# One cross attention of a twelve-layer decoder, rewritten as a single block with a turn per batch

## The reference, cut to what matters

```python
x = x + _L0_xattn_ref(_layernorm(x, axis=-1), ctx_768, L0_xattn_Wq, L0_xattn_Wk, L0_xattn_Wv, L0_xattn_Wout, L0_xattn_bout)

def _L0_xattn_ref(x, context, Wq, Wk, Wv, Wout, bout):
    HEADS = 8
    DIM_HEAD = 64
    SCALE = DIM_HEAD ** (-0.5)
    b, n, _ = x.shape
    m = context.shape[1]
    q = (x @ Wq).reshape(b, n, HEADS, DIM_HEAD)
    k = (context @ Wk).reshape(b, m, HEADS, DIM_HEAD)
    v = (context @ Wv).reshape(b, m, HEADS, DIM_HEAD)
    sim = jnp.einsum('bihd,bjhd->bhij', q, k) * SCALE
    attn = jax.nn.softmax(sim, axis=-1)
    out = jnp.einsum('bhij,bjhd->bihd', attn, v).reshape(b, n, HEADS * DIM_HEAD)
    return out @ Wout + bout
```

## Time and profile before

| what | us |
|---|---|
| median of 3 runs | 1572.71 (1567.17 to 1577.11) |
| profiled execution, whole time | 1575.55 |
| its span, first to last instruction | 1573.8 |
| PE busy in the span | 1303.9 (83%) |
| DVE, ACT, POOL busy | 730.2, 517.6, 405.9 |
| mean granted TensorE clock | 0.868 of full speed |
| stretch of the changed layer | 99.5 to 197.9 |

### The profile page before, as it was taken

The page is one execution under the profiler, slowest core; times in us unless marked ns, Lnnn a source line. Parts: engine busy times, 40 slices in busy tenths (PEclk is TensorE's granted clock), DMA queues, the critical chain, the costliest instruction groups (busy, mean ns, idle before and its releaser), DMA issues. The chain is left out here.

```text
span 1573.8 us, 26994 instructions
## 1 busy us (share of the span) xinstructions
PE 1303.9 (83%) x10492; PEld 950.1 (60%) x10492; DVE 730.2 (46%) x2172; ACT 517.6 (33%) x1216; POOL 405.9 (26%) x435
## 2 busy tenths in 40 slices
PE   4978839799968756887787799998959999983998
PEld 4866628588833433664465597785637774562676
DVE  4543374343479354663475414526841126655111
ACT  4523313344355312332342211312423324331332
POOL 5922288000053224740672120003010001030000
PEclk9998859899976676998898857998969989885999
DMA  3000040421091000000000000000021100000010
GB/s 126 1 4 0 0 174 1 132 70 55 2 279 36 1 29 0 1 1 1 0 1 1 8 2 1 1 3 2 1 73 40 40 12 1 3 1 27 28 40 27
DMA packets 46542, 48.28 MB, mean 31 GB/s; under 512 B 18944, under 2 KB 37888, under 8 KB 45536
## 3 DMA queue, kind: packets, MB, share of 16 engines
q1 hardware_dynamic: 46432, 46.76, 9.5%
HBM read 41.91 MB, written 4.85 MB: 30 GB/s over the span
## 5 line engine op out<-in xcount | busy, mean ns | idle before, releaser
L1156 PE MATMUL bank<-xnT,scratch 128*128 128x512 f32 x256 | 117.0, 606 | 15.6 <-DMA scratch<-e_l_ffn_w 15.6
L1217 DVE SCALAR_TENSOR_TENSOR x_res<-bank,scratch,x_res 128x128 f32<-128x128 f32 x128 | 36.0, 344 | 195.0 <-PE bank L1167 195.0
L1167 PEld LDWEIGHTS bank<-scratch 128*128 128x128 f32 x1024 | 118.1, 192 | 11.5 <-issue 11.5
L1196 ACT ACTIVATE scratch<-bank 128x512 f32<-128x512 f32 x128 | 76.5, 597 | 143.1 <-PE bank L1156 143.1
L1167 PE MATMUL bank<-scratch 128*128 128x128 f32 x1024 | 118.2, 275 | 0.0
L1156 PEld LDWEIGHTS bank<-xnT,scratch 128*128 128x128 f32 x256 | 48.0, 195 | 67.4 <-issue 66.4
L862 ACT ACTIVATE scratch<-bank 128x512 f32<-128x512 f32 x96 | 52.6, 594 | 93.7 <-PE bank L763 93.6
L821 DVE TENSOR_REDUCE scratch<-bank 128x4 f32<-128x512 f32 x96 | 63.1, 685 | 40.7 <-PE bank L2416 22.9
L2648 PE MATMUL bank<-weights,xnT 128*128 128x512 f32 x64 | 43.9, 787 | 23.7 <-DVE scratch L2757 21.4
L2641 POOL TENSOR_TENSOR scratch<-scratch 128x16 f32<-128x16 f32 x16 | 51.6, 3227 | 39.5 <-DVE scratch L2790 39.5
L827 DVE TENSOR_TENSOR scratch<-bank,scratch 128x512 f32<-128x512 f32 x96 | 61.3, 679 | 0.0
(11 more groups left out here) (527 smaller groups left out, 2896.3 us busy)
## 6 DMA issues: line engine op xcount, KB each, us to landing
scratch<-conv_kernels SPq DMA_DIRECT2D x8, 1024.0 KB, 11.0
scratch<-e_l_ffn_w SPq DMA_DIRECT2D x32, 256.0 KB, 2.8
scratch<-e_l_ffn_w SPq DMA_DIRECT2D x4, 1024.0 KB, 13.9
values<-scratch SPq DMA_DIRECT2D x8, 512.0 KB, 2.6
scratch<-values SPq DMA_DIRECT2D x8, 512.0 KB, 4.3
weights<-w_l_ffn SPq DMA_DIRECT2D x1, 3698.0 KB, 11.5
weights<-w_l_attn SPq DMA_DIRECT2D x1, 2560.5 KB, 9.0
weights<-w_l_attn SPq DMA_DIRECT2D x1, 2048.0 KB, 10.9
```

The costliest lines, as they stand in the source:

```text
L1156: nc.tensor.matmul(ps[m % 4][:, :], wa[s][:, i * P:(i + 1) * P], core.xnT[:, half * BANK:(half + 1) * BANK], start=True, stop=True) \
L1167: mm = nc.tensor.matmul(ps[4 + half][:, t * P:(t + 1) * P], hT[half][:, i, t * P:(t + 1) * P], wb[s][:, i, :], start=(i == 0), stop=(i == ...
L1196: nc.scalar.activation(hT[half][:, i, :], ps[m % 4][:, :], act_func, bias=bias2[:, s, i:i + 1] if b1 is not None else 0.0) \
```

## The change

The layer becomes one block with its own order, `NormInBlock` for the norm, and a turn per batch. Keys of the first four batches are projected first, from the context, while the norm runs; keys of the other four are projected one chunk a turn, queries of a pair in two fills, values of a batch in one fill with a column of ones beside each head. All fills, the output projection and the transposed output go through the two banks 4 and 5 in a fixed sequence, and ACT empties them in the same sequence. The output bias is laid out over 128 partitions on the host and added to x by POOL, which also adds each batch's projected output to x. The classes and functions that only the old form used are gone. Batch 0's values are in the opening list and, by `ahead(-1)`, once more in turn -1. Nothing else in the program changes.

```diff
-    layernorm_all(core, tag)
-    attention_by_pairs(core, tag, c, names_of(4, False, 4), heads, make, wq, wk, wv, wo, core.ctxT, CTX,
-                       K ** -0.5, bo=bo)
+    S_BANKS, T_BANKS, F_BANKS, O_BANKS = (0, 1), (2, 3), (4, 5), (6, 7)
...
+    TURNS = range(-1, B + 2)
+    first = [("k", 0, i) for i in range(CH)] + [("v", 0), ("q", 0, 0), ("q", 0, 1)]
+
+    def ahead(n):
+
+        fills = [("q", (n + 3) // 2, (n + 3) % 2)] if n + 3 < B else []
+        fills += [("k", 1, n + 1)] if n + 1 < CH else []
+        return fills + ([("v", n + 1)] if n + 1 < B else [])
...
+        @block.gpsimd
+        def _(pool):
+            nc.gpsimd.memset(vaug[:, :, :, K:K + 1], 1.0).then_inc(ones_set.sem, ones_set.up())
+            for h in range(2):
+                norm.pool(pool, h)
+            pool.wait_ge(*core.w_loaded[tag])
+            for h in range(2):
+                pool.wait_ge(norm.xn.sem, norm.batch(norm.xn, B // 2 * (h + 1) - 1))
+                xs = core.x[:, B // 2 * h:B // 2 * (h + 1), :]
+                nc.gpsimd.tensor_tensor(xs, xs, bo.unsqueeze(1).broadcast_to([P, B // 2, D]), ALU.add) \
+                    .then_inc(biased.sem, biased.up())
+            for b in range(B):
+                pool.wait_ge(biased.sem, biased.at(b // (B // 2)))
+                pool.wait_ge(emptied.sem, emptied.at(place["y", b]))
+                xs = core.x[:, b, :]
+                nc.gpsimd.tensor_tensor(xs, xs, y[:, b % 2, :], ALU.add).then_inc(added.sem, added.up())
...
+            def bank():
+                f = next(fills)
+                if f >= 2:
+                    pe.wait_ge(emptied.sem, emptied.at(f - 2))
+                return ps[F_BANKS[f % 2]]
...
+            for fill in first:
+                if fill == ("v", 0):
+                    norm.pe(pe, 0, O_BANKS[0])
+                if fill == ("q", 0, 0):
+                    pe.wait_ge(x_out.sem, x_out.at(0))
+                project(*fill)
+            norm.pe(pe, 1, O_BANKS[1])
+            for n in TURNS:
+                if 0 <= n < B:
+                    for par in range(2):
+                        pe.wait_ge(shifted.sem, shifted.at(2 * n + par))
+                        if n > 0:
+                            pe.wait_ge(exped.sem, exped.at(2 * (n - 1) + par))
+                        for i in range(CH):
+                            t = nc.tensor.transpose(ps[T_BANKS[par]][:, i * P:(i + 1) * P],
+                                                    shift[:, par, i * P:(i + 1) * P], core.ident[:, :])
+                        t.then_inc(turned.sem, turned.up())
+                if n + 1 < B:
+                    b = n + 1
+                    pe.wait_ge(emptied.sem, emptied.at(max(place["q", b // 2, 1], place["k", b // 4, CH - 1])))
+                    for i in range(CH):
+                        for par in range(2):
+                            t = nc.tensor.matmul(ps[S_BANKS[par]][:, i * P:(i + 1) * P],
+                                                 qT[rows(par), b // 2 % 2, i, b % 2 * P:(b % 2 + 1) * P],
+                                                 kT[rows(par), i, b * P:(b + 1) * P], start=True, stop=True)
+                            if i == CH - 1:
+                                t.then_inc(scores.sem, scores.up())
+                if 0 <= n - 2 < B:
+                    pe.wait_ge(emptied.sem, emptied.at(place["o", n - 2]))
+                    out = bank()
+                    for i in range(CH):
+                        t = nc.tensor.matmul(out[:, 0:D], oT[:, n % 2, i, :], wo[:, i, :], start=(i == 0), stop=(i == CH - 1))
+                    t.then_inc(filled.sem, filled.up())
+                for fill in ahead(n):
+                    if fill == ("q", 2, 0):
+                        pe.wait_ge(x_out.sem, x_out.at(1))
+                    project(*fill)
...
+                    for par in range(2):
+                        if n > 0:
+                            pe.wait_ge(normed.sem, normed.at(2 * (n - 1) + par))
+                        pe.wait_ge(exped.sem, exped.at(2 * n + par))
+                        for i in range(CH):
+                            t = nc.tensor.matmul(ps[O_BANKS[par]][:, i * (K + 1):(i + 1) * (K + 1)], prob[:, CH * par + i, :],
+                                                 vaug[:, n, 2 * i + par, :], start=True, stop=True)
+                        t.then_inc(valued.sem, valued.up())
...
-                           rows(g["L0_xattn_Wout"]), g["L0_xattn_bout"][None])
+                           rows(g["L0_xattn_Wout"]), every(g["L0_xattn_bout"]))
```

More of the change, by code:

```diff
@@ L505, in _, with project @@
[L505 to L511 removed]
+            fills = itertools.count()
+            def bank():
[3 more added lines that the diff above has]
+                return ps[F_BANKS[f % 2]]
+            def project(kind, n, m=0):
+                out = bank()
+                if kind == "k":
+                    t = nc.tensor.matmul(out[:, :], wk[0:CTX, m * P:(m + 1) * P], core.ctxT[0:CTX, half(n)],
+                                         start=True, stop=True)
+                elif kind == "v":
+                    t = nc.tensor.matmul(out[:, :], core.ctxT[0:CTX, n * P:(n + 1) * P], wv[0:CTX, :],
+                                         start=True, stop=True)
+                else:
+                    for i in range(2):
+                        t = nc.tensor.matmul(out[:, i * 2 * P:(i + 1) * 2 * P], wq[:, (2 * m + i) * P:(2 * m + i + 1) * P],
+                                             core.xnT[:, n * 2 * P:(n + 1) * 2 * P], start=True, stop=True)
+                t.then_inc(filled.sem, filled.up())
@@ L543, in _, with bank, empty @@
-            A.credit(act, "k0")
-            core.load_table(ACT.Exp)
-            act.wait_ge(*core.w_loaded[tag])
-            keys_out(-1)
-            A.credit(act, "v0")
-            values_out(-1)
-            turns(act, turn)
+            fills = itertools.count()
+            def bank():
+                f = next(fills)
+                act.wait_ge(filled.sem, filled.at(f))
+                return ps[F_BANKS[f % 2]]
+            def empty(kind, n, m=0):
+                src = bank()
+                if kind == "k":
+                    a = nc.scalar.copy(kT[:, m, half(n)], src[:, :])
+                elif kind == "v":
+                    a = nc.scalar.copy(vaug[:, n, :, 0:K], src[:, :].rearrange("p (h k) -> p h k", k=K))
+                else:
+                    a = nc.scalar.mul(qT[:, n % 2, 2 * m:2 * m + 2, :], src[:, :].rearrange("p (i t) -> p i t", i=2), K ** -0.5)
+                a.then_inc(emptied.sem, emptied.up())
@@ new lines, in _ @@
+            core.load_table(ACT.Exp)
+            for fill in first:
+                if fill == ("q", 0, 0):
+                    act.wait_ge(norm.turned.sem, norm.half(norm.turned, 0))
+                    nc.scalar.copy(core.xnT[:, half(0)], ps[O_BANKS[0]][:, :]).then_inc(x_out.sem, x_out.up())
+                empty(*fill)
+            for n in TURNS:
+                if 0 <= n < B:
+                    for par in range(2):
+                        act.wait_ge(turned.sem, turned.at(2 * n + par))
+                        nc.scalar.activation(prob[:, CH * par:CH * par + CH, :], by_head(ps[T_BANKS[par]][:, :]), ACT.Exp) \
+                            .then_inc(exped.sem, exped.up())
+                if 0 <= n - 2 < B:
+                    src = bank()
+                    if n - 2 >= 2:
+                        act.wait_ge(added.sem, added.at(n - 4))
+                    nc.scalar.copy(y[:, n % 2, :], src[:, 0:D]).then_inc(emptied.sem, emptied.up())
+                for fill in ahead(n):
+                    empty(*fill)
+                if 0 <= n - 1 < B:
+                    nc.scalar.copy(oT[:, (n - 1) % 2, :, :], by_head(bank()[:, :])).then_inc(emptied.sem, emptied.up())
```

367 lines of the change are left out of this document (67 added, 300 removed).

## The result

The changed kernel takes 1546.46 us in the median (1543.91 to 1549.45, four runs), the kernel before 1571.64 beside it (1567.17 to 1577.11, four runs): a ratio of 0.983, with a 95% interval from 0.9806 to 0.9853. A second measurement on another occasion gave 1548.33 against 1575.38, 0.9822 [0.9807, 0.9837]. The forecast was 1544, with a range from 1535 to 1554. The profiled execution took 1545.87 us (span 1544.1) against 1575.55 (1573.8), 29.7 less. The medians differ by 25.2 and 27.1.

What follows compares the result with a forecast made beforehand. The layer was taken as bounded by TensorE, its waits and its clock. Opening to 111.6, turns 46.9 and tail 9.5 gave 168.0 against 197.92; 29.5 us less, 1543.2 against the median, said as 1544, range 1535 to 1554.

Steps and rivals of the forecast that it cites:

- a turn becomes a stream on TensorE: Turns 0 to 6: TensorE steps without holes at granted clock 1.00, together 46.9 us.
- two rows: Old layer's turn: eight value instructions take 1.97 us after the hole, sixteen take 1.58 at full clock.
- The opening: Layer start: key fills beside the norm, first scores at 107.6, first transposes at 111.6; about 6 us gained.
- The double fill: Batch 0's v fill, in the opening and turn -1: 0.9 us in the sum, where TensorE would wait anyway.
- Fill waits: TensorE waiting for ACT to empty a fill bank: 25 fills by 0 to 0.3 us, taken near zero.
- the rival: Turns: every fill waits for ACT, 7.5 us, 1551; full waits with a cold opening, 1552 to 1557, 0.07.
- The tail: Turn 7, from the last batch's transposes to POOL's last add: 9.5 us.
- The 0.4 taken off for the next layer's start: Layer end: next layer starts 1.6 us after POOL, before 1.2 after DVE, so 29.9 becomes 29.5.
- Later layers: After the layer: nothing takes the gain back; absorbed or partly cold, 1558 to 1573 us, 0.06.
- The clock in the opening: Half clock until about 106 costs 3 to 4 us more; with full fill waits 1552 to 1557, 0.07.

Runs made afterwards that it cites:

- the two runs with filler: Unused products put where TensorE waits: in the kernel before (1571.26 us, ratio 0.9981) and in the kernel with late scores (1566.67 us, ratio 0.9942).
- the two kernels with late scores: Kernel after with scores of batch n+1 at the end of turn n, 1571.57 us; the second also with unused products ahead of the transposes, 1566.67 us.
- both with values once: Kernel after without the second product for batch 0's values in turn -1; two profiled executions, 1549.44 and 1537.21 us.
- both tightened: Kernel after with values once and two turns ahead, norm copy ahead of values' on ACT, transposed output before projection in last turn; 1548.24 us, ratio 0.9826.

## Why the prediction was right

**The mechanism.** That a turn becomes a stream on TensorE at granted clock 1.00 held. Start to start, expected and measured: 6.4 and 6.57, 6.8 and 7.02, 7.8 and 7.91, 6.9 and 6.96, 6.9 and 6.95, twice 6.05 and 6.09; together 46.9 and 47.6. The clock part was argued from two rows; the two runs with filler show it, 7.0 us in the old order and 10.8 in the late one, in one profile each. One reading behind it was wrong: that half clock makes the same work cost up to 2.5 times as much. The eight value instructions of 1.97 us take 1.09 at full clock, a factor of 1.8; the sixteen in 1.58 us that the prediction set beside them run at a faster pace (0.10 us each against 0.14) at the same full clock, so they are no fair measure. The sum didn't use that factor. And it says that TensorE has about as much to do, which leaves out the bias products that fell away; the sum, priced from the new kernel's own steps, isn't touched by it.

**The opening.** First transposes 12.78 us after the start, 12.1 expected. The query fills were to start 5.5 us after the block's start and started 6.2 after it (105.13): ACT copies the values of batch 0 first (104.01) and the normalized rows behind them (104.49), and TensorE waits 1.16 for that. Behind it all went as priced: 6.6 us from there to the first transposes, as in the forecast. In all the layer took 69.5 us from its first statistics to POOL's last add, in the forecast's 68 to 70, and 28.8 less up to the next layer where 29.5 were expected. Putting the keys first is worth up to 7.7 us, clock included, where the prediction put about 6 on the opening.

**The double fill.** The prediction has it both ways: 0.9 in the sum, and free because TensorE would wait anyway. It costs 0.53: the wait for DVE's first shift covers the other part of it.

**Fill waits.** Taken near zero, and they are zero: no row of PE's waits in the turns names a fill. The bound of 7.5 for the rival wasn't reached. The margin is thin, though: one bank less is 23.7 us, where the expectation of that run had about half, since it priced a wait of 0.8 for each fill behind a fill (0.94 measured) and no clock (up to 8.5).

**The tail** was 9.17 (9.5 expected). The 0.4 taken off for the next layer's start was wrong: it starts 1.24 us after POOL's last add, and before it was 1.2 behind DVE. PE's waits were to stay under 4 us, and do: 2.8 inside the layer, 4.3 with the stop at the block's start, which lies before it.

**Later layers.** Unchanged, as argued: 1374.67 and 1374.39. But the same instructions took 1366 to 1379 us in the other profiled executions, and that is the spread of the runs. The profiled execution of the kernel before stood 3.9 above its median (1575.55 and 1571.64), that of the kernel after 0.6 below (1545.87 and 1546.46), hence 29.7 between the profiles and 25 to 27 between the medians; the 28.7 that the forecast stands below 1572.71 lies between. Half clock in the opening, if the timed runs had it as most profiles do, would by itself make 25.5 to 27.2 of the 28.8; which of the two it is, spread or opening, no run shows.

**What was mis-sized.** The clock in the opening was put at 0.07 together with full fill waits. Eight profiles start the layer with the same four key fills into two banks. The clock was at 1.00 in three of these openings (the first profile of the kernel after and the two kernels with late scores) and below it in five (the second profile of the kernel after, both with values once, both tightened), so 1.6 or 3.3 us of it belong in the likeliest case, not in the range alone. That the profile set beside the forecast had a full clock there was luck of a few microseconds; the range would have held without it.

**Open.** What decides in one execution whether the opening runs at half clock isn't settled; the code and the 1.5 us stop are the same. And the timed runs of three kernels (filler in the old order, scores late, one fill bank) spread over 15 us with only one profile each, so whether their clock differs from run to run isn't shown.

## What to carry to other kernels

Where one engine does most of the work and a chain over three others must end before it can go on, look for work of the same engine that doesn't hang on the chain, and put it between: here moving eight score steps back behind the others gave up 27.7 of the layer's 28.8 us, with all the savings on the other engines kept. Price a hole on TensorE as the hole plus what the granted clock's row shows behind it; eight waits of 2.0 us cost 16.9 themselves and 10.8 more through the clock in the executions profiled, and waits of 0.7 in a row were followed by half clock as well. Give each fill a second bank before anything finer, and read a gain that is smaller than the runs' spread from the stretch of the layer in two or more profiles.

## What the hardware did that I had not expected

The granted clock fell to 0.50 with no wait of TensorE longer than 0.7 us in the 10 us before (one fill bank, at 135.60). The opening of the same layer ran at 1.00, 0.84 or 0.69 to 0.72 in executions of nearly the same code. A fill that waits for its only bank loses 0.26 us more than the wait that the row names. And one DVE instruction, of eight that otherwise take 0.34 us, took 1.36 where a POOL add of 1.26 began together with it (102.70).
